# Four buffers instead of two for gathered rows and index columns in the message passing layers of a graph network kernel

## The chip, the cores and the metric

The kernel runs on one core of a Trainium2 chip. The metric is the device time of one execution in microseconds. Before the change it is 11325.51 us, the median of 3 runs (11321.66 to 11331.46).

## What is computed

5000 nodes with 64 features, 165000 edges sorted by their target `dst`, each with 64 features `ea`. Four layers of message passing are followed by a weighted sum over edges. A layer of the reference, cut to what matters:

```python
def _genconv(x, src, dst, ea, W1, b1, lg, lb, W2, b2, t):
    m = relu(x[src] + ea) + EPS          # gather of 165000 rows of 64 floats
    logits = m * t
    mx = segment_max(logits, dst)
    e = exp(logits - mx[dst])
    denom = segment_sum(e, dst)
    agg = segment_sum(m * (e / denom[dst]), dst)
    h = (agg + x) @ W1 + b1
    return relu(_ln(h, lg, lb)) @ W2 + b2
...
ea = edge_attr @ eencW + eencb           # once, for all layers
for i in 1..3: x = x + _genconv(relu(_ln(x)), ...)
```

At the end a second part gathers once more, multiplies with edge weights and sums by target.

## The kernel before, in words

**Windows.** The edges are cut into two halves that are worked side by side (64 features of each half fill the 128 partitions). A window is 1536 edges of each half, 12 tiles of 128. A layer has 52 full windows (`FULLW`) and 4 small ones of half the width (`LAST`), 56 in all (`LW`). Within a window there are three groups (`NG`) of four tiles (`GT`). The number of a window counted over all layers is `g`, within a layer `w`, and `b` is its parity.

**What a window does.** GpSimd gathers the rows of `h_tab` by source with 24 indirect DMAs (12 tiles, 2 halves) into `xg[b]` (line 730), which tell of their landing in `xg_in[b][group]`. TensorE adds, group by group, `ea` times its weights (line 781) and the transposed gathered rows (line 785) in PSUM (`zl`) and counts `z_ps`; ScalarE makes `u` of each group (line 891) and then the logits in `zl` (line 895, `l_ok`). VectorE copies index columns (line 988), and runs the scans: running maximum forward (line 995), backward (line 996), the difference to the logits (line 1001, `diff_ok`), then, after ScalarE's exponentials (line 911), the scans for the denominator `den` (line 1007) and the numerator `num` (line 1011). TensorE transposes both back in six pieces through two PSUM banks (line 800), ScalarE copies each piece to `st_all` (line 903), and SyncE stores the window to `sums`. TensorE issues the forward part of window g+1 before the back part of window g (`layer`, line 804), and ScalarE keeps the same order.

**What GpSimd waits for.** The index columns of all windows lie in `idx_full`, but an indirect DMA takes its columns at a fixed address, so VectorE copies those of window w+2 into `idx[b]` at the start of its work on window w, and counts `idx_ok`. GpSimd waits for that count at the start of a window, and for `z_ps` of the window two before, group by group, which frees the rows' buffer. In the first layer the gathers of window 0 are issued in the block before, and those of window 1 at the start of the layer; in a later layer both wait for the new node table (`tab_out`). The small windows take their columns from `idx_last` and wait for `z_ps` alone.

**Node stage.** After the windows, GpSimd gathers the last sums of each node (`dn`, line 752, 40 indirect DMAs, `dn_in`), and the engines work the two small matrix products, 10 pieces of 4 tiles.

**Lists.** Before layer 0, VectorE also makes five lists for the last part (source, source by tiles, weights, and the two parts of an index), in tiles of their own (`src_i`, `src_n`, `wgt_n`, `lo_t`, `hi_t`); SyncE stores them (`out_lists`). VectorE waits for these stores before the node stage.

Of the kernel before, what the change touches and what calls it, by code (L numbers as in the profile page):

```python
# [25 lines left out]
I32 = mybir.dt.int32  # L26
# [55 lines left out]
def gnn(nc, x, src, dst, edge_attr, edge_weight, encW, encb, eencW, eencb, W1, b1, lnG, lnB, W2, b2,  # L82
# [16 lines left out]
    with ExitStack() as whole:  # L99
        def sb(name, shape, dt=F32, ctx=whole):  # L100
            return ctx.enter_context(nc.sbuf_tensor(name, shape, dt))[tuple([slice(None)] * len(shape))]

        def sem(name):
            return whole.enter_context(nc.semaphore(name))
# [38 lines left out]
        with ExitStack() as c:  # L143
# [60 lines left out]
            with nc.Block() as block:  # L204
                @block.sync
                def _(sp):
# [31 lines left out]
                    for a in acc:  # L238
                        sp.dma_start(a.rearrange("(p t) d -> p (t d)", p=P), zero[:, :]).then_inc(out_tabs, 16)
                    load_lists(2, 2, FULLW)  # L240
                    load_lists(FULLW, 0, 2)
                    sp.wait_ge(out_h, 16 * NC_CHUNK)
# [231 lines left out]
        with ExitStack() as c:  # L474
            xg.append(sb("xg1", [P, K, 2, D], F32, c))
            ea = [sb(f"ea{i}", [P, 2, K, D], F32, c) for i in range(2)]
            at = [sb(f"at{i}", [P, NG, GC], F32, c) for i in range(2)]
            turned = [e.rearrange("p h k d -> p (h k d)").rearrange("p (g c) -> p g c", c=GC) for e in ea]
            idx = [sb(f"idx{i}", [P, 2, K], I32, c) for i in range(2)]
            idx_ok = sem("idx_ok")  # L480
# [76 lines left out]
            XG_LAYER = 32 * GT * FULL_PAIRS + 32 * GT // 2 * (LAST // 2)  # L557

            def xg_count(l, i, gt):
                before = 32 * GT * i if gt == GT else 32 * GT * FULL_PAIRS + 32 * gt * (i - FULL_PAIRS)  # L560
                return l * XG_LAYER + before + 32 * gt

# [7 lines left out]
            with nc.Block() as block:  # L570
# [148 lines left out]
                def _(g_):  # L719

                    def window(g, w, l, b, gt=GT, small=None):
                        if small is None:
                            g_.wait_ge(idx_ok, l * FULLW + w + 1)
                            g_.sem_inc(gather_go, 1)
                        for k in range(NG * gt):
                            if k % gt == 0:
                                g_.wait_ge(z_ps, NG * g + k // gt + 1 - NG * 2 + Z0)
                                g_.sem_inc(gather_go, 1)
                            for h in range(2):
                                g_.indirect_dma_start(xg[b][:, k, h, :], None, h_tab[:, :], bass.IndirectOffsetOnAxis(  # L730
                                    ap=idx[b][:, h, k:k + 1] if small is None else idx_last[:, small, h, k:k + 1],
                                    axis=0)).then_inc(xg_in[b][k // gt], 16)

                    def layer(l):
                        if isinstance(l, int):
                            window(1, 1, l, 1)
                        else:
                            g_.wait_ge(tab_out, 16 * MC * l + 16)
                            g_.sem_inc(gather_go, 1)
                            for b in range(2):  # L740
                                window(l * LW + b, b, l, b)
                        with g_.Fori(1, FULL_PAIRS) as i:
                            for b in range(2):
                                window(l * LW + 2 * i + b, 2 * i + b, l, b)
                        g_.wait_ge(idx_last_in, 16 * LAST_LISTS)
                        for s in range(LAST):
                            window(l * LW + FULLW + s, None, l, s % 2, GT // 2, s)
                        for b in range(2):
# [11 lines left out]
                def _(pe):  # L760
# [3 lines left out]

                    def forward(g, i, l, b, gt=GT):
                        pe.wait_ge(ea_in[b], ea_count(l, i))
# [11 lines left out]
                        for gr in range(NG):  # L778
                            if first:
                                pe.wait_ge(at_sb, NG * g + gr + 1 + A0)  # L780
                            pe.matmul(ps[gr][:, 0:gt * P], attrW[:, :], (at if first else turned)[b][:, gr, 0:gt * P],  # L781
                                      start=True, stop=True)
                            pe.wait_ge(xg_in[b][gr], xg_count(l, i, gt))
                            for j in range(gt):
                                ins = pe.matmul(ps[gr][:, j * P:(j + 1) * P],  # L785
                                                xg[b][:, gr * gt + j, :, :].rearrange("p h d -> p (h d)"), ident[:, :],
                                                start=False, stop=True, skip_group_check=True)
# [16 lines left out]
                    def layer(l):  # L804
                        g0 = l * LW
                        forward(g0, 0, l, 0)
                        with pe.Fori(0, FULL_PAIRS - 1) as i:
                            forward(g0 + 2 * i + 1, i, l, 1)
                            back(g0 + 2 * i, 0)
                            forward(g0 + 2 * i + 2, i + 1, l, 0)  # L810
                            back(g0 + 2 * i + 1, 1)
                        forward(g0 + FULLW - 1, FULL_PAIRS - 1, l, 1)
                        back(g0 + FULLW - 2, 0)
                        for s in range(LAST):
                            forward(g0 + FULLW + s, FULL_PAIRS + s // 2, l, s % 2, GT // 2)
                            back(g0 + FULLW + s - 1, (s - 1) % 2, GT // 2 if s else GT)
# [158 lines left out]
                def _(v):  # L975

                    lists = idx_full.rearrange("p w h k -> p (w h k)")
                    v.wait_ge(idx_full_in, 32)
                    for b in range(2):
                        v.tensor_copy(idx[b].rearrange("p h k -> p (h k)"), lists[:, b * 2 * K:(b + 1) * 2 * K]).then_inc(idx_ok, 1)  # L980
# [8 lines left out]

                    def window(g, w, i, l, b, width=W):  # L990
# [77 lines left out]
                    with v.Fori(0, L) as l:  # L1068
# [14 lines left out]
                        v.tensor_scalar(tcur[:, 1:2], tcur[:, 0:1], EPS, None, ALU.mult).then_inc(tcur_ok, 1)  # L1083
                        with v.Fori(0, FULL_PAIRS) as i:
                            for b in range(2):
                                window(l * LW + 2 * i + b, 2 * i + b, i, l, b)
                        for s in range(LAST):
                            window(l * LW + FULLW + s, FULLW + s, FULL_PAIRS + s // 2, l, s % 2, W // 2)

# [21 lines left out]
                        base = MC * l  # L1111
                        v.wait_ge(out_lists, 16 * 5)
                        for k in range(MC + 3):
                            if k < MC:

                                cs = slice(k * MT, (k + 1) * MT)
                                v.wait_ge(dn_in[k], 16 * MT * (l + 1))
                                if k > 1:
# [493 lines left out]
```

## Time and profile before

| | |
|---|---|
| median of 3 runs | 11325.51 us |
| the profiled execution | 11249.37 us |
| its span | 11247.6 us |
| mean granted clock of TensorE | 0.682 |
| busy: PE 5127.0, DVE 5980.2, ACT 3007.5, POOL 6815.3 us | 46, 53, 27, 61% of the span |
| software queue (gathers), packets' share of 16 engines | 14.1% |
| hardware queue q1 | 22.4% |

Busy time is that of instructions; waits of an engine are the idle time before an instruction, with what ended it ("<-"). "remote" there means that the profile names no instruction as the one that ended the wait; "issue" that it shows no wait. PE is TensorE's matmuls, POOL is GpSimd. The layers lie between 200 and 9050 us, the last part between 9190 us and the end.

### The profile page before, as it was taken

What the parts mean: (1) busy time and instruction counts of PE and PEld (TensorE: products, weight loads), DVE (VectorE), ACT (ScalarE), POOL (GpSimd) and SP (SyncE); (2) the same over time, 40 slices, a digit from 0 to 9 for tenths busy, and PEclk for the clock granted to TensorE, in tenths of its full rate; (3) what the DMA queues carried; (4) which work ended last, traced back from release to release, by engine and by line L of the source; (5) the groups of instructions that cost most, each with busy time, mean ns of one, the idle gap of its engine ahead of it and who ended that gap; (6) DMA issues with size and microseconds to landing.
All of it is one profiled execution on the core that took longest, in us unless ns stands there. A gap on an engine that the chain in (4) does not pass through costs nothing. (4 is left out here: it accounts for less than half of the span.)

```text
span 11247.6 us, 87085 instructions
## 1 busy us (share of the span) xinstructions
PE 5127.0 (46%) x22750; PEld 3577.1 (32%) x22750; DVE 5980.2 (53%) x8070; ACT 3007.5 (27%) x4424; POOL 6815.3 (61%) x6468
## 2 busy tenths in 40 slices
PE   2444444443333332433333334333333358888887
PEld 2333323332222222322222223222222245555554
DVE  4443434443445444535444444444454458888887
ACT  1323223233233232323232323233332331111110
POOL 5554555545656666456666564656566538888887
PEclk8666566666666666666666666665666669999998
DMA  5332333332333333323333332233333335555554
GB/s 137 108 101 97 110 99 99 110 117 57 100 94 104 95 102 87 103 69 104 95 102 97 94 105 76 85 96 103 94 104 95 99 89 97 96 92 97 96 94 83
DMA packets 780499, 1091.38 MB, mean 97 GB/s; under 512 B 501054, under 2 KB 543664, under 8 KB 778660
## 3 DMA queue, kind: packets, MB, share of 16 engines
q1 hardware_dynamic: 453902, 862.82, 22.4%
q0 software_dynamic: 322624, 224.55, 14.1%
q10 hardware_dynamic: 3916, 3.40, 0.1%
q8 instruction: 20, 0.33, 0.0%
q14 instruction: 37, 0.30, 0.0%
HBM read 610.39 MB, written 479.85 MB: 97 GB/s over the span
## 5 line engine op out<-in xcount | busy, mean ns | idle before, releaser
L730 POOL DMA_INDIRECT xg<-h_tab,idx x4968 | 4765.1, 959 | 3546.9 <-DVE idx L988 1870.3
L988 DVE COPY idx<-idx_full 128x24 int32 x208 | 37.6, 181 | 4040.2 <-ACT zl L895 4022.3
L800 PE MATMUL turn<-ident,den 128*128 128x128 f32 x2592 | 492.2, 334 | 3307.1 <-ACT st_all L903 3170.1
L1293 POOL DMA_INDIRECT acc<-vm,tgt x1026 | 1597.6, 1557 | 374.1 <-issue 299.6
L891 ACT ACTIVATE u<-zl,attrB 128x512 f32<-128x512 f32 (+1 forms) x672 | 746.5, 1122 | 3347.6 <-remote 2720.9
L800 PEld LDWEIGHTS turn<-ident,den 128*128 128x128 f32 x2592 | 393.0, 221 | 3357.2 <-ACT st_all L903 3214.9
L785 PEld LDWEIGHTS zl<-ident,xg 128*128 128x128 f32 x5184 | 971.7, 254 | 1122.5 <-issue 993.5
L785 PE MATMUL zl<-ident,xg 128*128 128x128 f32 x5184 | 980.8, 336 | 609.7 <-issue 506.0
L781 PE MATMUL zl<-ea,attrW 128*128 128x512 f32 (+1 forms) x1008 | 752.6, 840 | 793.9 <-DVE rx L1001 751.2
L903 ACT ACTIVATE st_all<-turn 128x512 f32<-128x512 f32 (+1 forms) x1344 | 746.8, 577 | 494.7 <-PE turn L800 324.6
L1542 DVE TENSOR_TENSOR spreadz<-turn,hi_hot 128x2560 f32<-128x2560 f32 x270 | 762.7, 2825 | 65.0 <-ACT gh L1427 26.0
L1366 PE MATMUL zl<-spreadz,lo_hot 128*128 128x512 f32 x1620 | 768.4, 611 | 50.1 <-DVE spreadz L1542 50.1
L995 DVE TENSOR_TENSOR_SCAN rx<-rp,carry,zl 128x1536 f32<-128x1536 bf16 (+1 forms) x224 | 739.8, 3303 | 34.0 <-ACT zl L895 31.7
L1007 DVE TENSOR_TENSOR_SCAN den<-keep,start,rx 128x1536 f32<-128x1536 bf16 (+1 forms) x224 | 739.0, 3299 | 30.3 <-DVE start L1005 0.2
L1011 DVE TENSOR_TENSOR_SCAN num<-keep,start,rx 128x1536 f32<-128x1536 bf16 (+1 forms) x224 | 739.0, 3299 | 7.8
L996 DVE TENSOR_TENSOR_SCAN segmax<-rp,rx 128x1536 f32<-128x1536 bf16 (+1 forms) x224 | 725.6, 3239 | 7.6
L800 PE MATMUL turn<-ident,num 128*128 128x128 f32 x2592 | 599.1, 405 | 100.7 <-issue 70.7
L800 PEld LDWEIGHTS turn<-ident,num 128*128 128x128 f32 x2592 | 485.3, 223 | 178.3 <-ACT st_all L903 80.4
L1366 PE MATMUL rx<-spreadz,lo_hot 128*128 128x512 f32 x1080 | 507.5, 592 | 0.0
L781 PEld LDWEIGHTS zl<-ea,attrW 128*128 128x128 f32 x1008 | 220.0, 271 | 850.5 <-issue 446.8
L781 PE MATMUL zl<-at,attrW 128*128 128x512 f32 (+1 forms) x336 | 290.4, 949 | 381.1 <-ACT at L885 311.1
L885 ACT ACTIVATE at<-turn 128x512 f32<-128x512 f32 (+1 forms) x168 | 93.1, 575 | 1302.0 <-remote 1169.4
(259 smaller groups left out, 7340.9 us busy)
## 6 DMA issues: line engine op xcount, KB each, us to landing
sums<-st_all SPq DMA_DIRECT2D x208, 1536.0 KB
ea<-feat SPq DMA_DIRECT2D x158, 768.0 KB
srcB<-src_flat SPq DMA_DIRECT2D x108, 768.0 KB
rp<-run_pen SPq DMA_DIRECT2D x210, 384.2 KB
xg<-h_tab,idx POOLq DMA_INDIRECT x4968
run_head<-zeros SPq DMA_DIRECT2D x216, 192.0 KB
hd<-run_head SPq DMA_DIRECT2D x108, 384.0 KB
ea<-in_edge_attr_dram SPq DMA_DIRECT2D x104, 384.0 KB
```

Of the source, the lines that this page charges most:

```text
L730: g_.indirect_dma_start(xg[b][:, k, h, :], None, h_tab[:, :], bass.IndirectOffsetOnAxis(ap=idx[b][:, h, k:k + 1] if small is None else idx ...
L781: pe.matmul(ps[gr][:, 0:gt * P], attrW[:, :], (at if first else turned)[b][:, gr, 0:gt * P], start=True, stop=True)
L785: ins = pe.matmul(ps[gr][:, j * P:(j + 1) * P], xg[b][:, gr * gt + j, :, :].rearrange("p h d -> p (h d)"), ident[:, :], start=False, stop= ...
L800: ins = pe.transpose(ps[6 + (b + r) % 2][:, j * P:(j + 1) * P], sum_v[:, gr * gt + j, :], ident[:, :])
L891: a.activation(u[b][:, 0:width].rearrange("c (p k) -> c k p", k=NG * gt)[:, gr * gt:(gr + 1) * gt, :], ps[gr][:, 0:gt * P].rearrange("c (k ...
L903: a.activation(st[b].rearrange("p h k c -> p k h c")[:, gr * gt:(gr + 1) * gt, :, s_ * D:(s_ + 1) * D], ps[6 + (b + r) % 2][:, 0:gt * P].r ...
L995: link(v.tensor_tensor_scan(rx[:, 0:width], rp[b][:, 0:width], zl[:, 0:width], carry[:, 0:1], ALU.min, ALU.max))
L1007: v.tensor_tensor_scan(den[b][:, 0:width], keep[b][:, 0:width], rx[:, 0:width], start2[:, 0:1], ALU.mult, ALU.add).then_inc(den_ok, 1)
L1011: v.tensor_tensor_scan(num[b][:, 0:width], keep[b][:, 0:width], rx[:, 0:width], start2[:, 1:2], ALU.mult, ALU.add).then_inc(sums_ok, 1)
L1293: g_.indirect_dma_start(acc[i][:, :], bass.IndirectOffsetOnAxis(ap=tgt[b][:, t_:t_ + 1], axis=0), vm[b][:, t_, :], None, compute_op=ALU.ad ...
L1366: ins = pe.matmul(bank[:, :], lo_hot[b][:, n, :], z[:, part * 512:(part + 1) * 512], start=False, stop=True, skip_group_check=True)
L1542: v.tensor_tensor(spreadz[(XT * b + n) % 2][:, :, :], rows_bank[2][:, at_:at_ + D].unsqueeze(1).broadcast_to([P, NT, D]), hi_hot[b][:, n, ...
```

## The change

The tiles for gathered rows and for index columns become four each (`DEPTH`). VectorE copies the columns of window w+4 at the start of window w, GpSimd waits for `z_ps` of the window four before, gathers windows 1 to 3 at the start of layer 0 and windows 0 to 3 at that of a later layer, and the loops of TensorE, VectorE and GpSimd cover four windows a turn in place of two. `ea`, `rp`, `u`, `den`, `num` and the store's buffers stay double. The room for it comes from the five lists' tiles, which now lie in `segmax`, `den` and `num`; so the wait for the lists' stores moves from the node stage to the point before the first `den` scan of every window. The ten semaphores of the node rows are taken from the twelve of the gathered rows, with their counts added.

```diff
+        DEPTH = 4
-        idx_full = sb("idx_full", [P, FULLW + 2, 2, K], I32)
+        idx_full = sb("idx_full", [P, FULLW + DEPTH, 2, K], I32)
-        xg_in = [[sem(f"xg_in{i}_{gr}") for gr in range(NG)] for i in range(2)]
+        xg_in = [[sem(f"xg_in{i}_{gr}") for gr in range(NG)] for i in range(DEPTH)]
...
-                    load_lists(0, 0, 2)
+                    load_lists(0, 0, DEPTH)
...
-            xg.append(sb("xg1", [P, K, 2, D], F32, c))
+            xg += [sb(f"xg{i}", [P, K, 2, D], F32, c) for i in range(1, DEPTH)]
-            idx = [sb(f"idx{i}", [P, 2, K], I32, c) for i in range(2)]
+            idx = [sb(f"idx{i}", [P, 2, K], I32, c) for i in range(DEPTH)]
...
-            src_i = sb("src_i", [ROWS, W], I32, c)
-            src_n = sb("src_n", [ROWS, W], F32, c)
-            wgt_n = sb("wgt_n", [ROWS, W], F32, c)
+            src_i = segmax[0:ROWS, :].bitcast(I32)
+            src_n = den[0][0:ROWS, :]
+            wgt_n = den[1][0:ROWS, :]
...
-            lo_t = sb("lo_t", [ROWS, W], F32, c)
-            hi_t = sb("hi_t", [ROWS, W], F32, c)
+            lo_t = num[0][0:ROWS, :]
+            hi_t = num[1][0:ROWS, :]
...
-            dn_in = [sem(f"dn_in{i}") for i in range(MC)]
...
-            Z0, U0, L0, M0, S0, BP0, BS0, A0, D0 = 2 * NG, NG, 2, 2, 2, 2 * BU, BU + 1, 2, 1
+            Z0, U0, L0, M0, S0, BP0, BS0, A0, D0 = DEPTH * NG, NG, 2, 2, 2, 2 * BU, BU + 1, 2, 1
...
+            dn_in = [xg_in[n // NG][n % NG] for n in range(MC)]
...
                         for k in range(NG * gt):
                             if k % gt == 0:
-                                g_.wait_ge(z_ps, NG * g + k // gt + 1 - NG * 2 + Z0)
+                                g_.wait_ge(z_ps, NG * g + k // gt + 1 - NG * DEPTH + Z0)
...
-                        if isinstance(l, int):
-                            window(1, 1, l, 1)
-                        else:
+                        if not isinstance(l, int):
                             g_.wait_ge(tab_out, 16 * MC * l + 16)
                             g_.sem_inc(gather_go, 1)
-                            for b in range(2):
-                                window(l * LW + b, b, l, b)
-                        with g_.Fori(1, FULL_PAIRS) as i:
-                            for b in range(2):
-                                window(l * LW + 2 * i + b, 2 * i + b, l, b)
+                        for b in range(1 if isinstance(l, int) else 0, DEPTH):
+                            window(l * LW + b, b, l, b)
+                        with g_.Fori(1, FULLW // DEPTH) as i:
+                            for b in range(DEPTH):
+                                window(l * LW + DEPTH * i + b, DEPTH * i + b, l, b)
...
                         if width == W:
-                            next_lists(w + 2, b)
+                            next_lists(w + DEPTH, place)
...
                         v.wait_ge(back_ps, BU * (g - 1) + BP0)
+                        v.wait_ge(out_lists, 16 * 5)
                         v.tensor_tensor_scan(den[b][:, 0:width], keep[b][:, 0:width], rx[:, 0:width], start2[:, 0:1],
                                              ALU.mult, ALU.add).then_inc(den_ok, 1)
```

## Rows read from the trace of the kernel before

**Rows 1.** The page's costliest groups: count, busy us, mean ns, idle before, releaser.
```profile
L730 POOL DMA_INDIRECT xg<-h_tab,idx x4968 | 4765.1, 959 | 3546.9 <-DVE idx L988 1870.3
L988 DVE COPY idx<-idx_full 128x24 int32 x208 | 37.6, 181 | 4040.2 <-ACT zl L895 4022.3
```

**Rows 2.** Stretches, layers 0 and 1: us; busy (count) PE, PEld, DVE, ACT, POOL; PEclk, DMA, GB/s.
```profile
201.50:2502.00 2300.50, 1025.23 (x5407) 758.39 (x5408) 983.01 (x726) 687.38 (x886) 1194.46 (x1248) 0.63 0.33 104
2662.00:4682.90 2020.90, 670.52 (x2894) 501.20 (x2895) 983.07 (x724) 612.92 (x721) 1210.05 (x1265) 0.62 0.33 98
```

**Rows 3.** Timeline of one window in layer 1: start us, duration, what.
```profile
3029.86 0.18 DVE L988 COPY idx<-idx_full 128x24 int32 x1 [17.91 <-ACT zl L895]
3031.03 0.96 POOL L730 DMA_INDIRECT xg<-h_tab,idx  x1 [7.91 <-DVE idx L988]
...
3042.67 1.16 ACT L891 ACTIVATE u<-zl,attrB 128x512 f32<-128x512 f32 x1 [0.97 <-PE zl L785]
...
3045.69 1.05 PE L785 MATMUL zl<-ident,xg 128*128 128x128 f32 x8
...
3060.05 0.95 POOL L730 DMA_INDIRECT xg<-h_tab,idx  x1 [0.30 <-issue]
3064.75 1.14 ACT L891 ACTIVATE u<-zl,attrB 128x512 f32<-128x512 f32 x1 [11.46 <-remote]
...
3067.73 0.18 DVE L988 COPY idx<-idx_full 128x24 int32 x1 [17.91 <-ACT zl L895]
```

**Rows 4.** Timeline of ScalarE, back part of a window near layer 1's end.
```profile
4480.85 0.60 ACT L903 ACTIVATE st_all<-turn 128x512 f32<-128x512 f32 x1 [9.90 <-remote]
...
4500.45 0.60 ACT L903 ACTIVATE st_all<-turn 128x512 f32<-128x512 f32 x1 [7.80 <-remote]
...
4516.84 0.60 ACT L903 ACTIVATE st_all<-turn 128x512 f32<-128x512 f32 x1 [0.36 <-PE turn L800]
```

**Rows 5.** Timelines of GpSimd, VectorE and ScalarE at the start of layer 2.
```profile
4802.07 1.27 POOL L730 DMA_INDIRECT xg<-h_tab,idx  x1 [62.79 <-issue]
...
4840.94 3.45 DVE L995 TENSOR_TENSOR_SCAN rx<-rp,carry,zl 128x1536 f32<-128x1536 bf16 x1
...
4892.00 0.96 POOL L730 DMA_INDIRECT xg<-h_tab,idx  x1 [0.31 <-issue]
...
4893.18 1.15 ACT L891 ACTIVATE u<-zl,attrB 128x512 f32<-128x512 f32 x1 [25.44 <-remote]
...
4906.08 3.42 DVE L995 TENSOR_TENSOR_SCAN rx<-rp,carry,zl 128x1536 f32<-128x1536 bf16 x1
```

**Rows 6.** Stretches, one full window (w50 of layer 1).
```profile
4591.30:4611.40 20.10, 10.80 (x50) 7.99 (x49) 18.06 (x15) 10.89 (x12) 10.84 (x12) 0.75 0.46 149
```

**Rows 7.** Stretches, layer 1: w46 to w49; w47; w49; w46 to the end.
```profile
4433.10:4591.30 158.20, 53.30 (x225) 38.70 (x226) 72.26 (x53) 46.25 (x55) 97.72 (x103) 0.61 0.30 94
4463.60:4515.20 51.60, 14.07 (x64) 10.32 (x65) 18.01 (x14) 12.90 (x17) 24.43 (x26) 0.60 0.23 70
4536.00:4591.30 55.30, 16.66 (x63) 11.89 (x64) 17.98 (x14) 12.33 (x16) 36.64 (x40) 0.56 0.26 72
4433.10:4682.90 249.80, 99.21 (x426) 74.94 (x427) 147.73 (x126) 89.81 (x128) 137.82 (x144) 0.65 0.36 108
```

**Rows 8.** Stretches, layer 0: w47 to the end; 44 windows in its middle.
```profile
2267.10:2502.00 234.90, 117.50 (x661) 91.68 (x662) 130.07 (x115) 88.95 (x139) 114.86 (x120) 0.68 0.39 122
332.00:2267.00 1935.00, 854.81 (x4472) 628.76 (x4472) 794.51 (x570) 559.96 (x700) 1008.43 (x1054) 0.62 0.32 103
```

**Rows 9.** Timeline of VectorE, last small window of layer 1.
```profile
4671.66 1.82 DVE L995 TENSOR_TENSOR_SCAN rx<-rp,carry,zl 128x768 f32<-128x768 bf16 x1
4682.93 0.22 DVE L1092 CUSTOM_DVE_ANT_0 wjunk<-wmax,win_hot 128x56 f32<-128x56 f32 x1 [0.20 <-DVE carry L1015]
```

**Rows 10.** Timeline at the start of layer 0.
```profile
202.54 0.95 POOL L730 DMA_INDIRECT xg<-h_tab,idx  x1 [26.28 <-DVE idx L988]
...
212.46 3.41 DVE L1007 TENSOR_TENSOR_SCAN den<-keep,start,rx 128x1536 f32<-128x1536 bf16 x1 [0.15 <-DVE start L1005]
```

More of the change, by code:

```diff
@@ L239, in _ @@
                         sp.dma_start(a.rearrange("(p t) d -> p (t d)", p=P), zero[:, :]).then_inc(out_tabs, 16)
-                    load_lists(2, 2, FULLW)
-                    load_lists(FULLW, 0, 2)
+                    load_lists(DEPTH, DEPTH, FULLW)
+                    load_lists(FULLW, 0, DEPTH)
                     sp.wait_ge(out_h, 16 * NC_CHUNK)
@@ L551, in gnn, with xg_count, dn_count @@
             LAST_LISTS = sum(E - h * HALF - FULLW * W - s * W // 2 > 0 for s in range(LAST) for h in range(2))
-            Z0, U0, L0, M0, S0, BP0, BS0, A0, D0 = 2 * NG, NG, 2, 2, 2, 2 * BU, BU + 1, 2, 1
+            Z0, U0, L0, M0, S0, BP0, BS0, A0, D0 = DEPTH * NG, NG, 2, 2, 2, 2 * BU, BU + 1, 2, 1
             PAIRS = LW // 2
             FULL_PAIRS = FULLW // 2
[L557 to L561, printed above, removed]
+            XG_LAYER = 32 * GT * FULLW // DEPTH + 32 * GT // 2 * LAST // DEPTH
+            dn_in = [xg_in[n // NG][n % NG] for n in range(MC)]
+            def xg_count(l, turn_, gt, n):
+                before = 32 * GT * turn_ if gt == GT else 32 * GT * FULLW // DEPTH
+                return l * (XG_LAYER + (16 * MT if n < MC else 0)) + before + 32 * gt
+            def dn_count(l):
+                return (l + 1) * (XG_LAYER + 16 * MT)
             def ea_count(l, i):
@@ L734, in layer @@
                     def layer(l):
-                        if isinstance(l, int):
-                            window(1, 1, l, 1)
-                        else:
+                        if not isinstance(l, int):
                             g_.wait_ge(tab_out, 16 * MC * l + 16)
                             g_.sem_inc(gather_go, 1)
-                            for b in range(2):
-                                window(l * LW + b, b, l, b)
-                        with g_.Fori(1, FULL_PAIRS) as i:
-                            for b in range(2):
-                                window(l * LW + 2 * i + b, 2 * i + b, l, b)
+                        for b in range(1 if isinstance(l, int) else 0, DEPTH):
[3 more added lines that the diff above has]
+                                window(l * LW + DEPTH * i + b, DEPTH * i + b, l, b)
                         g_.wait_ge(idx_last_in, 16 * LAST_LISTS)
                         for s in range(LAST):
-                            window(l * LW + FULLW + s, None, l, s % 2, GT // 2, s)
+                            window(l * LW + FULLW + s, None, l, s, GT // 2, s)
                         for b in range(2):
@@ L763, in _, with forward @@
                     pe.sem_inc(back_ps, BP0)
-                    def forward(g, i, l, b, gt=GT):
+                    def forward(g, i, l, b, turn_, place, gt=GT):
                         pe.wait_ge(ea_in[b], ea_count(l, i))
@@ L782, in forward @@
                                       start=True, stop=True)
-                            pe.wait_ge(xg_in[b][gr], xg_count(l, i, gt))
+                            pe.wait_ge(xg_in[place][gr], xg_count(l, turn_, gt, NG * place + gr))
                             for j in range(gt):
                                 ins = pe.matmul(ps[gr][:, j * P:(j + 1) * P],
-                                                xg[b][:, gr * gt + j, :, :].rearrange("p h d -> p (h d)"), ident[:, :],
+                                                xg[place][:, gr * gt + j, :, :].rearrange("p h d -> p (h d)"), ident[:, :],
                                                 start=False, stop=True, skip_group_check=True)
@@ L805, in layer @@
                         g0 = l * LW
[L806 to L813, printed above, removed]
+                        forward(g0, 0, l, 0, 0, 0)
+                        with pe.Fori(0, FULLW // DEPTH - 1) as i:
+                            for n in range(1, DEPTH + 1):
+                                forward(g0 + DEPTH * i + n, DEPTH // 2 * i + n // 2, l, n % 2, i + n // DEPTH, n % DEPTH)
+                                back(g0 + DEPTH * i + n - 1, (n - 1) % 2)
+                        for n in range(FULLW - DEPTH + 1, FULLW):
+                            forward(g0 + n, n // 2, l, n % 2, n // DEPTH, n % DEPTH)
+                            back(g0 + n - 1, (n - 1) % 2)
                         for s in range(LAST):
-                            forward(g0 + FULLW + s, FULL_PAIRS + s // 2, l, s % 2, GT // 2)
+                            forward(g0 + FULLW + s, FULL_PAIRS + s // 2, l, s % 2, None, s, GT // 2)
                             back(g0 + FULLW + s - 1, (s - 1) % 2, GT // 2 if s else GT)
@@ L978, in _ @@
                     v.wait_ge(idx_full_in, 32)
-                    for b in range(2):
+                    for b in range(DEPTH):
                         v.tensor_copy(idx[b].rearrange("p h k -> p (h k)"), lists[:, b * 2 * K:(b + 1) * 2 * K]).then_inc(idx_ok, 1)
@@ L988, in next_lists, with window @@
                         v.tensor_copy(idx[b].rearrange("p h k -> p (h k)"), lists[:, bass.ds(w * 2 * K, 2 * K)]).then_inc(idx_ok, 1)
-                    def window(g, w, i, l, b, width=W):
+                    def window(g, w, i, l, b, place, width=W):
                         link = Chain(v, dve_step, g * STEPS)
@@ L1083, in _ @@
                         v.tensor_scalar(tcur[:, 1:2], tcur[:, 0:1], EPS, None, ALU.mult).then_inc(tcur_ok, 1)
-                        with v.Fori(0, FULL_PAIRS) as i:
-                            for b in range(2):
-                                window(l * LW + 2 * i + b, 2 * i + b, i, l, b)
+                        with v.Fori(0, FULLW // DEPTH) as i:
+                            for n in range(DEPTH):
+                                window(l * LW + DEPTH * i + n, DEPTH * i + n, DEPTH // 2 * i + n // 2, l, n % 2, n)
                         for s in range(LAST):
-                            window(l * LW + FULLW + s, FULLW + s, FULL_PAIRS + s // 2, l, s % 2, W // 2)
+                            window(l * LW + FULLW + s, FULLW + s, FULL_PAIRS + s // 2, l, s % 2, None, W // 2)
                         v.wait_ge(dve_step, (l + 1) * LW * STEPS)
@@ L1111, in _ @@
                         base = MC * l
-                        v.wait_ge(out_lists, 16 * 5)
                         for k in range(MC + 3):
@@ L1116, in _ @@
                                 cs = slice(k * MT, (k + 1) * MT)
-                                v.wait_ge(dn_in[k], 16 * MT * (l + 1))
+                                v.wait_ge(dn_in[k], dn_count(l))
                                 if k > 1:
```

## The prediction

> **What bounds the kernel now.** I read the page's groups first, then the stretches, then the timeline of one window, and then the places where the timeline departs from its pattern. The group of the gathers [rows 1] shows GpSimd busy for 4765 us and idle for 3547 us before gathers, 1870 us of it "released by" the DVE copy of index columns (L988). Layer 0 takes 2300.5 us from its first scan to its last window, layer 1 takes 2020.9 [rows 2], and layers 2 and 3 are like layer 1; together some 8360 of 11248 us, so this is where the change acts.
>
> One window in the middle of layer 1 lasts 37.9 us [rows 3]. At 3029.86 DVE copies the index columns; 1.2 us later GpSimd begins 24 gathers, one every 1.264 us, and issues the last at 3060.05 (30.3 us in all); then it is idle for 7.9 us until the next copy. The copy at the start of window w hands over the columns of w+2, so the gathers of this stretch are for the window after next. The next window's rows already lie in the other buffer. PE shows this: it issues that window's group 2 at 3045.69, in the middle of the stream. But ScalarE reads group 0 at 3042.67 and group 2 only at 3064.75, 19 us after PE issued it, with "remote" as releaser, while ScalarE, DVE and PE have nothing else to do. The logits and the next copy at 3067.73 follow. The last u starts 3.7 us after the end of the last gather's issue (3060.05 + 0.96). So the chain of a window is: copy, 1.2 us, gather stream 30.3 us, 3.7 us, u and logits 3.0 us, copy.
>
> Why does a window wait for gathers that it doesn't read? The same happens where gathered rows play no part. In the transposes of sums (L800), PE's results reach ScalarE in 0.3 to 0.4 us when no gathered rows are landing, and 8 to 10 us apart while GpSimd streams: ScalarE's idle time before st_all is 9.90 and 7.80 us in one stretch (a piece between them is the same), 0.36 us in a quiet one [rows 4]. My reading: while gathered rows land, what PE has finished is reported late, and what is pending comes out mostly when the stream pauses. The page "TensorE: Matmul & The Clock Gate" of the Trainium skill, section "The cost: per-tile semaphore tail", has PE's increments cost about 26 ns each; rows 4 disagree by two orders of magnitude in the stream and agree only outside it. By that page nothing would hold the windows but GpSimd, which is rival D below.
>
> The start of a layer shows a stream with no pause [rows 5]. GpSimd starts at 4802.07 and streams three windows (w0, w1, w2) to 4892.96. Window 0's scan starts at 4840.94, but the second piece of window 1's u comes at 4893.18, after 25.44 us of waiting and just as the stream ends, and the scan at 4906.08: 65.1 us for one window. A window whose passes meet few gathers takes 20.1 us [rows 6]. So streaming further ahead isn't free: it is paid in late windows while it lasts.
>
> **The change, part by part.** (1) Four buffers and four index columns. The copy in window w hands over w+4, and GpSimd waits for z_ps of w rather than of the window two back from its own target; both are again "window w has passed". In the steady state the ring is full, GpSimd waits for the copy of window w, and that copy starts one window of gathers (w+4 in place of w+2). The chain of rows 3 is the same term by term: 1.2 + 30.3 + 3.7 + 3.0, 38 us. It is worth nothing there. I bound it: at most the 7.9 us of idle per window (rival D), and at worst the stop-and-go pattern (rival E).
>
> (2) The start of layers 1 to 3. GpSimd now issues w0 to w3 at once, and w4 as soon as window 0 has passed: the stream ends (k+4) x 30.33 us after its start, if window k is the one whose end it must await. Window k then can be held until about 8 us after it (6.7 us in rows 3, 13.1 us in rows 5). Before, scans start 38.9 and 104.0 us [rows 5] after the first gather, then every 37.9 us. For k = 1: 160 against 104, 56 us late; k = 2: 190 against 142, 48; k = 3: 221 against 180, 41; k = 6: 311 against 294, 18. Which k depends on how fast windows pass in a stream; rows 5 have one in 65 us, and the stretches with a stream in most of them 51.6 and 55.3 us [rows 7]. At 65 us window 2 would pass at 169 and window 3 at 234, past the 221 of k = 3; I take 45 us, between k = 2 and 3.
>
> (3) The end of each layer. GpSimd is two windows further ahead, so it finishes earlier and two more windows run at 20.1 in place of 37.9. From the scan of w47: gathers of w51 to 31.5 us, two groups of the first small window to 41.6, 6.7 us to the next scan, 48; then four windows at 20 and four small ones at 11.3 (layer 1's last, [rows 9]): 173 us. The small windows' gathers (15 us each) start when a z group is done and fall beside DVE's scans, as at 4591 to 4611, where one took 20.1 us with 12 gathers in it. Before, from the scan of w46, 249.8 us [rows 7]; now 37.9 + 173 = 211, so 39 us are won. Bounds: 0 and 50.
>
> (4) Layer 0. GpSimd gathers w1 until 176.3 us and is then idle for 26.3 us until the first copy [rows 10]. Now w2 and w3 follow at once and stream to 237; window 0's z groups fall into that stream. Window 0 can be held to 245 (44 us late), window 1 to 275 against 241 (34 us). I take 35. At the end, from w47's scan 234.9 us before [rows 8]; now some 54 + 4 x 21 + 4 x 13 = 190 (an estimate: the terms of (3), each with a little of the 6 us that a window of layer 0 takes longer), 45 us less. Together -10.
>
> (5) The wait for the list stores, now before the first den scan, which began at 212.46 [rows 10]: it is met long before in later windows, and DVE waits for the logits in each. Were it late in window 0 alone, it would cost what the stores need, 0 to 10 us once; I take 0. Scratch in the rooms of sums and maxima moves no instruction. Two more columns loaded early and two more copies of 0.18 us: nothing. Shared semaphores for node rows: same transfers, same order. Longer loop bodies: ScalarE's and SyncE's keep two windows; no row prices the others, I take 0, with 0 to 10 us per layer.
>
> The sum: 3 x (45 - 39) - 10 = +8 us on the profiled execution's 11249.4 us. That execution is 76 us faster than the runs' median of 11325.5, which says that the irregular stretches vary between executions; I carry the difference over: 11334 us, said as 11335.
>
> **The rivals.** What a measurement can tell from no change is 0.2%, 23 us.
> B, slower: the start decides. If PE's results hardly come out in a stream, window 1 is held until GpSimd has filled the ring (k = 1 in layers 1 to 3, k = 0 in layer 0): 3 x (56 - 39) + (44 - 45) = +50, 11376 us; with the win at the end halved it is +131, 11456. It decides from 47 us of start cost per layer on. For it: the 25.44 us before a piece of u in the unbroken stream of rows 5. Against: pieces 8 to 11 us apart in rows 4.
> C, somewhat faster: windows pass in about 45 us in the stream, so that the ring fills slowly (k = 6): 3 x (18 - 39) + (0 - 45) = -108, 11217 us. For it: 51.6 and 55.3 us were mostly stream, not wholly bad. Against: 65.1.
> D, much faster: GpSimd's issue becomes the bound, 30.3 us a window, no idle time before copies: 46 windows x 3 x 7.6, and 46 x 13.7 in layer 0 (whose middle windows take 1935.0 / 44 = 44.0 us [rows 8]), 1680 us less, 9645 us. It needs PE's lateness to be something that goes when the gathers are further ahead, say a wait for the rows themselves. For it: the 1870 us in rows 1, read plainly. Against: rows 4, where no gathered row is read, and PE's own group 2 issued at 3045.69.
> E, slower by a pattern: four windows near the end of layer 1, two of them 51.6 and 55.3 us, make 158.2 for 4 x 37.9 = 151.6 [rows 7]; were it the rule with more room to run ahead, 208 / 4 x 6.6 = +343, 11669 us.
> That the change doesn't do what it says (the ring never used beyond two) would be exactly the old time and belongs to the forecast.
>
> **How the numbers follow.** Forecast 0.33, B 0.30, C 0.18, D 0.10, E 0.09. The likeliest case's own range is 11290 to 11380. Within 23 us of before lies 0.27 (most of the forecast and the edges of B and C); slower 0.38 (B, E and a piece of the forecast's upper side, less B's lower edge); faster 0.35 (C, D and the forecast's lower side). The range, 11215 to 11460, takes in B with the halved gain and C, and leaves out D and E, about 2 in 10.
>
> **What the profile after would show.** Right: middle windows again 37.9 us (44 in layer 0), idle time before gathers about as before and still put down to the copy of index columns, group 2's u still some 3.7 us after the stream's end; at the layers' starts one stream of six or so windows with windows 1 to 3 taking 50 to 75 us each; at the ends four or five windows of 20 us in a row. The forecast falls if middle windows shrink towards 30.3 us, if u's idle time "remote" (L891) vanishes, or if the starts cost less than 20 us or more than 60. The window-0 wait is wrong if DVE stands before den at 212 us.

## The result: 0.63% slower, and two kinds of chip

The changed kernel takes 11402.78 us (median of 4 runs, 11399.75 to 11406.66) against 11328.49 us (4 runs): ratio 1.0063, 95% interval 1.005 to 1.0076, 74 us slower. Its profiled execution takes 11400.83 us (span 11399.1), 2 us from its median; that of the old kernel was 76 us below its own.

The experiments brought a second result. On three chips the old kernel took 9127.8 to 9137.4 us, on two others 11321.3 and 11323.7, each in at least 7 runs that lay within 0.3%. I call the latter kind A; the runs above are of it by their times. The others are kind B. There the changed kernel is 0.17% faster. Each of the five chips showed one kind in all its executions, but four of them in one sitting only, so a lasting state of a chip is not told from the chip itself. What follows first is kind A.

**The profile after.** The page's groups, as in [rows 1], with the group of u; columns: count, busy us, mean ns, idle before, releaser:

```profile
L734 POOL DMA_INDIRECT xg<-h_tab,idx x4968 | 4760.8, 958 | 3537.2 <-DVE idx L990 1873.6
L990 DVE COPY idx<-idx_full 128x24 int32 x208 | 37.7, 181 | 4103.3 <-ACT zl L897 3928.1
L893 ACT ACTIVATE u<-zl,attrB 128x512 f32<-128x512 f32 (+1 forms) x672 | 750.8, 1122 | 3379.9 <-remote 2557.9
```

GpSimd's idle time is in total what it was (3546.9 us before), and has the same releaser. Twice the buffers took 10 us from it. One window in layer 2 answers to [rows 3]:

```profile
5224.92 0.18 DVE L990 COPY idx<-idx_full 128x24 int32 x1 [18.32 <-ACT zl L897]
5226.09 0.95 POOL L734 DMA_INDIRECT xg<-h_tab,idx  x1 [8.09 <-DVE idx L990]
...
5237.73 1.15 ACT L893 ACTIVATE u<-zl,attrB 128x512 f32<-128x512 f32 x1 [0.96 <-PE zl L787]
...
5241.15 1.05 PE L787 MATMUL zl<-ident,xg 128*128 128x128 f32 x8
...
5250.23 1.14 ACT L893 ACTIVATE u<-zl,attrB 128x512 f32<-128x512 f32 x1 [11.35 <-remote]
...
5255.06 0.95 POOL L734 DMA_INDIRECT xg<-h_tab,idx  x1 [0.30 <-issue]
5260.07 1.15 ACT L893 ACTIVATE u<-zl,attrB 128x512 f32<-128x512 f32 x1 [8.70 <-remote]
5263.05 0.18 DVE L990 COPY idx<-idx_full 128x24 int32 x1 [18.11 <-ACT zl L897]
```

Copy, 1.2 us, 24 gathers, 4.1 us, last u, logits, copy: 38.1 us. The second piece of u comes 12.5 us after the first, the third 9.8 us after that. The start of layer 1 answers to [rows 5]; timelines of all engines:

```profile
2633.78 0.95 POOL L734 DMA_INDIRECT xg<-h_tab,idx  x1 [64.25 <-issue]
...
2658.95 1.15 ACT L893 ACTIVATE u<-zl,attrB 128x512 f32<-128x512 f32 x1 [8.93 <-PE zl L787]
...
2671.64 1.14 ACT L893 ACTIVATE u<-zl,attrB 128x512 f32<-128x512 f32 x1 [11.54 <-issue]
...
2700.42 1.14 ACT L893 ACTIVATE u<-zl,attrB 128x512 f32<-128x512 f32 x1 [13.95 <-PE zl L787]
...
2727.02 1.14 ACT L893 ACTIVATE u<-zl,attrB 128x512 f32<-128x512 f32 x1 [25.46 <-issue]
...
2755.72 1.14 ACT L893 ACTIVATE u<-zl,attrB 128x512 f32<-128x512 f32 x1 [27.55 <-remote]
...
2778.12 0.60 ACT L905 ACTIVATE st_all<-turn 128x512 f32<-128x512 f32 x1 [11.30 <-remote]
2778.77 1.13 PE L802 MATMUL turn<-ident,num 128*128 128x128 f32 x4 [10.76 <-issue]
...
2788.62 0.60 ACT L905 ACTIVATE st_all<-turn 128x512 f32<-128x512 f32 x1 [9.90 <-remote]
...
2801.43 1.91 PE L783 MATMUL zl<-ea,attrW 128*128 128x512 f32 x2
...
2815.52 0.95 POOL L734 DMA_INDIRECT xg<-h_tab,idx  x1 [0.30 <-issue]
...
2837.12 2.96 ACT L893 ACTIVATE u<-zl,attrB 128x512 f32<-128x512 f32 x3 [12.13 <-remote]
...
2841.92 0.18 DVE L990 COPY idx<-idx_full 128x24 int32 x1 [8.89 <-ACT zl L897]
2842.01 3.42 DVE L997 TENSOR_TENSOR_SCAN rx<-rp,carry,zl 128x1536 f32<-128x1536 bf16 x1
2842.32 1.14 PE L802 MATMUL turn<-ident,den 128*128 128x128 f32 x4 [4.56 <-ACT st_all L905]
2843.09 0.95 POOL L734 DMA_INDIRECT xg<-h_tab,idx  x1 [26.61 <-DVE idx L990]
```

GpSimd streams six windows without waiting for a copy, 2633.8 to 2816.5, and then waits 26.61 us for the copy. The last two pieces of window 0's u are 12.7 us apart, those of window 1's 27 and 29; those of st_all, which has fewer matmuls in a piece, 10.5 to 12. The stretches, columns as in [rows 2]: layer 1 from its first gather to window 2's scan, on to w47's scan (45 windows), and to its end; layer 0 to window 2's scan, and from w47's scan to its end:

```profile
2633.80:2842.00 208.20, 36.77 (x120) 24.24 (x120) 39.44 (x33) 27.09 (x27) 139.10 (x144) 0.54 0.18 42
2842.00:4562.20 1720.20, 563.68 (x2430) 421.58 (x2430) 814.51 (x586) 513.35 (x586) 1030.90 (x1080) 0.61 0.32 98
4562.20:4741.80 179.60, 87.47 (x372) 67.61 (x373) 129.59 (x114) 79.24 (x115) 68.72 (x72) 0.68 0.39 121
100.50:331.80 231.30, 47.78 (x268) 34.31 (x268) 91.15 (x130) 31.84 (x36) 149.77 (x144) 0.57 0.42 113
2326.20:2512.30 186.10, 108.76 (x660) 86.94 (x661) 129.52 (x113) 90.16 (x139) 68.70 (x72) 0.71 0.44 146
```

### The profile page after: what moved, and what is told of

It reads as the page before. It is cut to its first block and busy times, and to the rows that moved or that the text cites. A ratio compares the mean times of both kernels' runs of the same rounds, so it can differ in the third digit from the quotient of the medians.

```text
span 11399.1 us, 86751 instructions
## 1 busy us (share of the span) xinstructions
PE 5130.5 (45%) x22750; PEld 3585.2 (31%) x22750; DVE 5970.2 (52%) x8072; ACT 3009.9 (26%) x4424; POOL 6809.2 (60%) x6468
## 5 line engine op out<-in xcount | busy, mean ns | idle before, releaser
L990 DVE COPY idx<-idx_full 128x24 int32 x208 | 37.7, 181 | 4103.3 <-ACT zl L897 3928.1
L1010 DVE TENSOR_TENSOR_SCAN den<-keep,start,rx 128x1536 f32<-128x1536 bf16 (+1 forms) x224 | 739.0, 3299 | 44.3 <-issue 35.3
L1368 PEld LDWEIGHTS zl<-spreadz,lo_hot 128*128 128x128 f32 x1620 | 299.3, 199 | 366.7 <-issue 272.9
```

Of the source, the lines that this page charges most:

```text
L1368: ins = pe.matmul(bank[:, :], lo_hot[b][:, n, :], z[:, part * 512:(part + 1) * 512], start=False, stop=True, skip_group_check=True)
```

## The experiments

**One part at a time: how far GpSimd runs ahead.** Buffers and loop bodies stay as changed. Two windows ahead is this edit, in the first copies of index columns, the later ones, and the count that GpSimd waits for; three and one have a 3 and a 1 in it.

```
-                    for b in range(DEPTH):
+                    for b in range(2):
-                            next_lists(w + DEPTH, place)
+                            next_lists(w + 2, (place + 2) % DEPTH)
-                                g_.wait_ge(z_ps, NG * g + k // gt + 1 - NG * DEPTH + Z0)
+                                g_.wait_ge(z_ps, NG * g + k // gt + 1 - NG * 2 + Z0)
```

> The changed kernel with its four buffers, loop bodies and waits, but GpSimd runs only two windows ahead again: the copy in window w hands over w+2, and both the first copies and GpSimd's wait for z_ps count two windows. Theory T (what PE has finished is reported late while gathered rows land, so running further ahead costs at each start and pays at each end): the old time, 11330 us (11310 to 11345); windows after a layer's first scan 64 and 38 us, layer ends two windows at 20 us again. Rival F (the new form costs: longer loop bodies, one more wait in each window, shared semaphores): stays at 11380 to 11410.

Measured: 9137.92 us beside an old kernel of 9129.07, ratio 1.001 (1.0001 to 1.0019). It landed on kind B, so neither number of the expectation could be met, and nothing followed for the 74 us. The same holds for the next three.

> As the run with two windows ahead, but three. T: between them, 11350 to 11380 us: starts of layers 1 to 3 some 30 to 35 us longer than with two, ends about 18 us per layer shorter, middle windows 38 us. Rival F: 11380 to 11410, the same for two, three and four.

Measured: 9114.49, ratio 0.9984 (0.9975 to 0.9993).

Waiting once for the stores of the lists, ahead of the loop over layers, in place of in window() before the den scan:

```
-                        v.wait_ge(out_lists, 16 * 5)
+                    v.wait_ge(out_lists, 16 * 5)
```

> The changed kernel, with the wait for the list stores once ahead of the layers in place of once in each window. Forecast's step 5 (that wait costs nothing): 11403 us within 10, middle windows 38.2 us as now. Rival: the wait carries the 0.25 us by which middle windows grew (38.2 against 37.95): then some 11 us per layer go, 11355 to 11365 us.

Measured: 9126.82, ratio 0.9996 (0.9987 to 1.0005), beside 0.9983 with the wait in the window (below). VectorE's timeline of this run:

```profile
178.51 0.06 DVE L1073 MEMSET carry<- 128x1 f32 x1 [8.33 <-DMA hi_tile<-num]
...
194.63 0.18 DVE L990 COPY idx<-idx_full 128x24 int32 x1 [12.10 <-ACT zl L897]
```

DVE stands 8.33 us at the wait, and the first scan comes at 194.7 us where the changed kernel has it at 185.7. In the window the wait is met when VectorE comes to it: in the changed kernel DVE is idle for 0.22 us before the first den on kind B and on kind A alike (0.15 us before the change [rows 10]), and before all 224 den scans together for 44.3 us where the old kernel's page has 30.3. That is 14 us more in four layers, so the rival's 11 us in each can't be idle time of that wait, even on kind A, where this edit was not run.

Rows two windows ahead, index columns four (only the third pair of lines of the edit above):

> The changed kernel with its index columns four windows ahead, but GpSimd's wait for z_ps counts two windows: rows of w+2 are gathered as soon as w's z group is reported, not after w's logits. If the late copy were what held GpSimd (the 1874 us of its idle time put down to it), windows go to 30 to 33 us and the kernel below 10500 us. T: GpSimd's stream then comes in three pieces of 10 us, each held by a z group that the piece before it makes late: 13 + 14 + 14 us, 38 to 42 us a window, 11300 to 12100 us.

Measured: 9134.5, ratio 1.0004 (0.9995 to 1.0013). On kind B neither what holds the rows nor what holds the lists matters to middle windows, 30.2 us here too. But the changed kernel's 0.17% is gone with the rows' lead: it goes with rows four windows ahead, not with index columns.

**The changed and the old kernel on kind B.**

> The changed kernel as it is, once more, because in the four runs before the old kernel took 9129 us in place of 11328. Theory T2 (whether PE's results are late in a gather stream depends on the chip, not on the kernel): where the old kernel takes some 9130 us, its windows take 30.3 us, which is GpSimd's issue, and the change makes no difference: ratio 0.998 to 1.001; where the old kernel takes some 11330 us, the ratio is 1.006 again. Rival: the change costs 70 us wherever it runs (the form of the code), ratio 1.008.

Measured: 9122.02 against 9137.35, ratio 0.9983 (0.9974 to 0.9992): as the theory had it for this kind, against the rival's 1.008.

> The old kernel itself, for its profile on a chip where it takes some 9130 us. T2 (GpSimd's issue is the bound there): all full windows of layers 1 to 3 at 30.3 us, GpSimd with next to no idle time within them, 3 windows of some 23 us at the start of layer 0 where the changed kernel has 6; the 15 us between the two kernels lie in layer 0. Should the time be 11330 us, the profile is the first one's again, with windows of 38 us.

Measured: 9129.27, ratio 1.0 (0.9989 to 1.0012). The middle of layer 1 in this run, and its groups:

```profile
1956.50:3316.30 1359.80, 710.06 (x2430) 496.02 (x2430) 814.13 (x587) 512.77 (x586) 1030.70 (x1081) 0.63 0.42 124
```

```profile
L730 POOL DMA_INDIRECT xg<-h_tab,idx x4968 | 4752.6, 957 | 1628.1 <-issue 1584.4
L785 PE MATMUL zl<-ident,xg 128*128 128x128 f32 x5184 | 1200.4, 405 | 1552.7 <-DMA xg<-h_tab,idx 1541.7
...
L891 ACT ACTIVATE u<-zl,attrB 128x512 f32<-128x512 f32 (+1 forms) x672 | 758.3, 1128 | 2620.9 <-PE zl L785 2620.6
```

45 windows in 1359.8 us are 30.2 us each: GpSimd's issue. The idle time before the gathers that was put down to the copy of index columns is gone, PE waits for the rows to land, and "remote" has vanished before u. What the change can win here is the start of layer 0. GpSimd's timelines, old kernel and changed kernel; the listed rows are those with an idle time of over 1 us before them:

```profile
120.90 0.95 POOL L730 DMA_INDIRECT xg<-h_tab,idx  x1 [6.83 <-DVE idx L980]
187.86 0.95 POOL L730 DMA_INDIRECT xg<-h_tab,idx  x1 [27.20 <-DVE idx L988]
```

```profile
121.37 0.96 POOL L734 DMA_INDIRECT xg<-h_tab,idx  x1 [6.84 <-DVE idx L982]
```

The 27.20 us are gone, and window 6 is scanned at 324.7 us in place of 346.5. Layers 1 to 3 give back 3.7, 4.8 and 5.3 us (1652.8, 1653.9 and 1654.7 from first gather to last window, against 1649.1, 1649.1 and 1649.4).

**Taking away half of the gathers.**

```
-                            for h in range(2):
+                            for h in range(2 if small is not None else 1):
                                 g_.indirect_dma_start(xg[b][:, k, h, :], ...
```

Not shown: the counts that PE and VectorE wait for follow it, and the buffers are zeroed once before layer 0. The kernel leaves out the second half's rows.

> The changed kernel with 12 gathers in a full window in place of 24 (the second half's rows aren't gathered; small windows and all other work stay). GpSimd's stream is then 15.2 us a window. If the chip is one on which the old kernel takes some 9130 us and GpSimd's issue is the bound: windows fall to 20.1 us (23 in layer 0), the time of a window without that bound, some 7280 us. If it is one on which it takes some 11330: T gives 15.2 + 7.7 = 23 us a window (29 in layer 0), some 8400 us; a rival in which the lateness doesn't depend on gathers leaves windows at 38.

Measured, on kind B: 7235.07, ratio 0.7923 (0.7909 to 0.7936). Windows of 20.1 to 21 us (20.45 on average) and 22 to 23.7 in layer 0, as said.

**One window ahead.**

> The changed kernel with GpSimd one window ahead. On a chip of 9130 us: nothing lies between a window's last gather and the window any more, and the chain is copy, 1.2, 30.3, landing 2.4, PE 1.1, u 1.1, logits 1.6 = 37.7 us: +7.4 a window, some 10600 us. On a chip of 11330 us, T: windows take the same chain already, 38 us as with two and four, starts of layers shorter by some 28 us and ends longer by 18: 11300 us within 60; a rival in which work done in the stream counts: 45 to 50 us a window, over 12500 us.

Measured, on kind B: 10710.43, ratio 1.1728 (1.1709 to 1.1748); all middle windows 37.7 us, the sum of the chain as worked out; the total is 110 us over what was said. One buffer of lead hides the gathers behind nothing; with two everything but GpSimd's issue is hidden, and a third and fourth have nothing left to hide.

**Four windows ahead in layer 0, two later.**

```
-                                g_.wait_ge(z_ps, NG * g + k // gt + 1 - NG * DEPTH + Z0)
+                                g_.wait_ge(z_ps, NG * g + k // gt + 1 - NG * (DEPTH if isinstance(l, int) else 2) + Z0)
                             g_.wait_ge(idx_ok, l * FULLW + w + 1)
+                            if not isinstance(l, int):
+                                g_.wait_ge(l_ok, g - 2 + 1 + L0)
```

> The changed kernel, GpSimd four windows ahead in layer 0 and two from layer 1 on (it waits there for the logits of the window two back). On a chip of 9130 us: as the changed kernel, ratio 0.998, since what the change wins there is in layer 0, where GpSimd doesn't stand idle before window 0's copy. On a chip of 11330 us, T: layers 1 to 3 as in the old kernel (2061 to 2070 us), layer 0 as in the changed one (+10): 11340 us, ratio 1.001.

Measured, on kind B: 9111.43, ratio 0.998 (0.997 to 0.999), the number expected: the win is layer 0's. It was not run on kind A.

**The same kernels on kind A.** First two windows ahead:

> The changed kernel with GpSimd two windows ahead once more, sent because the runs so far all had the old kernel at 9129 to 9137 us. Should the old kernel take some 11330 us beside it, T (the depth of running ahead costs at the starts) expects ratio 1.000 to 1.002 and layer starts of 64 and 38 us, rival F (the form costs) 1.005 to 1.008. Beside an old kernel of 9130 us it repeats the first ratio, 1.001, and tells nothing of the 11330 us.

Measured: 11332.89 (11325.67 to 11338.55) against 11323.65, ratio 1.0009 (1.0 to 1.0019). The changed kernel had 1.0063. Rival F's 1.005 to 1.008 is out: of the 0.63%, 0.54% (61 us) go with the depth alone. A small price of the form is left: this same kernel has 1.0009 here and 1.001 (1.0001 to 1.0019) on kind B. The start of layer 1 to window 2's scan and from w47's scan to the end, in this run:

```profile
2644.70:2788.60 143.90, 32.54 (x120) 22.79 (x120) 39.52 (x35) 27.55 (x27) 93.48 (x96) 0.58 0.21 51
4504.10:4722.90 218.80, 90.45 (x372) 69.29 (x373) 129.82 (x113) 78.93 (x115) 114.74 (x120) 0.62 0.37 106
```

Next to the changed kernel's stretches: 208.2 against 143.9, 64.3 us lost at the start; 179.6 against 218.8, 39 us won at the end.

> 12 gathers in a full window in place of 24, once more (second half's rows not gathered), for a chip on which the old kernel takes 11330 us. There, T (PE's results wait for gathered rows to stop landing): a window is its stream of 15.2 us and the 7.7 us behind it, 23 us, some 29 in layer 0, 8400 us in all. Rival (the lateness has nothing to do with the gathers): windows of 38 us, 11300 us. Rival (half the landings are few enough that nothing is late): 20.3 us, 7300 us. On a chip of 9130 us it repeats 7235.

Measured: 8040.19, ratio 0.7102 (0.7088 to 0.7116). The middle of layer 1:

```profile
1888.70:2888.20 999.50, 554.52 (x2430) 416.13 (x2430) 815.18 (x586) 503.78 (x586) 515.30 (x540) 0.70 0.46 151
```

45 windows of 22.2 us, 27.4 in layer 0: the stream of 15.2 us and 7.0 behind it, 0.8 less than said; the total is 360 us less than said. The rival of 38 us is out: with half of the gathers the late windows go. The one of 20.3 us misses by 1.9 us, T by 0.8, and since the same kernel has 20.45 on kind B, the middle windows tell these two apart by little. The layer's start does it better: the scans of windows 0 and 1 are 66.1 us apart here and 20.1 on kind B. So at both lengths tried the stream and some 7 to 8 us behind it make a middle window of layers 1 to 3 on kind A.

> GpSimd one window ahead, once more, for a chip on which the old kernel takes 11330 us. There, T with nothing of use done in a stream: windows of 38 us as with two and four, starts of layers 28 us shorter than with two, ends 18 longer: 11300 us within 60. Rival, that a window's passes use the stream (some 12 of its 20 us beside it): 45 to 50 us a window, over 12500 us. On a chip of 9130 us it repeats 10710.

Measured: 11376.7 (11358.92 to 11377.06), ratio 1.0044 (1.0027 to 1.006), 17 us over the upper end of T's 11300 within 60. Start, middle and end of layer 1:

```profile
2663.00:2777.80 114.80, 39.21 (x120) 25.48 (x120) 39.70 (x34) 27.48 (x27) 70.58 (x72) 0.60 0.23 57
2777.80:4505.90 1728.10, 754.33 (x2430) 501.68 (x2430) 814.32 (x587) 511.17 (x586) 1033.68 (x1080) 0.59 0.32 97
4505.90:4750.70 244.80, 105.84 (x372) 74.66 (x373) 129.87 (x114) 79.33 (x115) 137.84 (x144) 0.60 0.34 98
```

The start is 29.1 us shorter than with two, as expected, the end 26.0 longer (18 expected), and 0.28 us more per middle window makes 12.7. The windows of 38.4 us don't support T by themselves: on kind B the same kernel has 37.7, from the chain of landing rows.

For layers 1 to 3 the depth is then priced on kind A, all in the same form of the kernel (us, from the scans):

```
windows ahead   first gather to w2's scan   w47's scan to the end   layer 0, first gather to end
1               114.8 114.6 114.4           244.8 248.9 250.7       2442.9
2               143.9 145.2 145.1           218.9 218.8 218.2       2422.8
4               208.2 209.3 209.3           179.5 181.3 175.4       2411.8
```

Two is the best of them on kind A; no version that ran beats the old kernel there, and on kind B three, four and the mixed one beat it by 0.16 to 0.2%.

## Why the prediction was right in part

The time, 11402.78, lies in the range given and 68 us above the number; it is outside the likeliest case's own range (11290 to 11380) and in rival B's, 11376 to 11456. B was the case of a start that costs more than 47 us per layer; it did. B's own way there (window 1 held until the ring is full, k = 1) isn't what happened: window 1 passes within the stream, and window 2 is held. So the number lies near B's by another way.

**The steady state, part (1)**: right. 38.1 to 38.2 us, put down to the same copy, the last u 4.1 us after the stream.

**The start of layers 1 to 3, part (2), is the step that failed.** It had 45 us; against the same form with two windows ahead it is 64 (64.3, 64.1 and 64.2), against the old kernel's profile 66 to 67 (141.9 to window 2's scan in each of its layers). The stream's length was right: (2 + 4) x 30.33 = 182 us for k = 2, and it took 182.7. Two terms were wrong. The smaller is which window is held: I took 45 us as the cost, between the 48 of k = 2 and the 41 of k = 3, going by 65.1 us for a window in a stream [rows 5]. The stream's end had cut that window short; in the long stream it takes 84.1 (2674.7 to 2758.8), so it is window 2. That is 3 us. The larger is what comes behind the stream: I had window 2 pass "about 8 us after it", and it passed 25.5 us after it, which is the other 18.

The reading behind it was not sharp enough. I had PE's results "reported late", with no price. In the long stream the gaps scale with the matmuls in a piece, not with the reports: a piece of u is 2 + 8 matmul instructions, a piece of st_all 4 (x2, x8, x4 in the rows above), and they come 26.6 to 28.7 us and 10.5 to 11.9 us apart: 2.6 to 3.0 us a matmul in both. The 25.44 us of waiting in the old kernel [rows 5], with the some 1.2 us of the piece before it, are the same rate. The PE rows give another picture (x8 in 1.05 us), but by what ScalarE is given, PE works off one matmul per some 2.7 us there. It isn't the price wherever rows land: window 0's last pieces at the head of the same stream are 12.7 us apart (18.5 and 17.0 in layers 2 and 3), and the first two of a middle window 12.5 (above): 1.3 to 1.9 us a matmul at most, beside gathers issued at the same pace. Why it rises later in a stream was not tried. With the 2.7 us, taken from this profile and so after the fact, the term comes out: window 1's 30 matmuls are 81 us (84.1 with the rest of the window); window 2 has the 24 transposes of window 0 ahead of its own 30, 146 us, more than the 57.7 left of the stream, so it passes behind it, with nearly all of its 30 still to do. All three pieces can be read some 15 us after the last st_all (2821.6 to 2837.1), half a us a matmul, so what was held is worked off once the stream is over. Whether PE is slow in starting, reading or finishing them isn't told apart.

**The end, part (3)**: right. 39 us; measured 39.4, 37.5 and 42.8. From w47's scan 173; measured 175 to 181.

**Layer 0, part (4)**: the net is right, -10 against -11.0, and both halves are 10 us larger: +44.7 at the start (231.3 against 186.6 to window 2's scan) and -55.8 at the end (186.1 from w47's scan, where the text had 190, against 241.9 with two windows ahead, where it had 234.9).

**Part (5)**: right within its bounds. The wait finds its stores done. The form costs 0.09% on kind A, 9 us, at the edge of its interval.

With these terms the sum is 3 x (64 - 40) - 11 = +61 us, the 0.54% between the two depths; the form's 9 us make it 70 of the 74. Carrying over the 76 us by which the old kernel's profiled execution was fast was right: 11321 to 11328 in all comparisons on kind A. Its middle windows had 37.8 to 37.9 us, while both kernels of the new form have 38.2; whether the old one has 38.2 in an ordinary execution wasn't seen.

**Rival D** (GpSimd's issue as the bound, 30.3 us a window) is false on kind A and describes kind B well, but there it is the state of the old kernel too, and not something that the change brings. I had not thought of the chip as a condition. The rule weighed there (the Trainium skill, "TensorE: Matmul & The Clock Gate", "The cost: per-tile semaphore tail": some 26 ns per increment) is likewise at odds with kind A's rows only: on kind B transposes reach their reader in 0.26 us beside a stream (last rows below). No run measures an increment itself, on either kind.

## What to carry to other kernels

Deeper prefetch is worth something only where the prefetching engine stands idle for want of a buffer in its steady state: if its idle time has the same releaser with the ring full, more depth moves the irregular ends alone, and starts and ends are to be priced apart. When results reach their reader in slow steps, count the instructions in each step before calling it latency, and check the price in a second place: here 2.7 us a matmul fits two kinds of pieces in a long stream, and not those at its head. And a verdict of under one per cent belongs to the chips it was taken on: this one changes its sign between them.

## What was unexpected in the hardware

Two groups of chips run one program 24% apart (11321 to 11328 against 9128 to 9137 us), each steady within 0.3%. The transfers' packets don't take longer: the rows on gathered rows' queue, old kernel, kind A and then kind B,

```profile
q0 software_dynamic: 322624, 224.55, 14.1%
```

```profile
q0 software_dynamic: 322624, 224.55, 17.2%
```

make 0.141 x 11247.6 = 1586 us and 0.172 x 9128.6 = 1570 us of the 16 engines' time. The clock granted to PE in middle windows is the same too (0.62 in [rows 2], 0.63 on kind B). What differs is PE's work beside landing rows. On kind B, at the start of layer 2 (old kernel, ScalarE's timeline), window 1's three pieces of u are 6.9 and 7.7 us apart, where kind A has 27 to 29, and a transposed piece comes 0.26 us after the one before it was read:

```profile
3640.46 1.16 ACT L891 ACTIVATE u<-zl,attrB 128x512 f32<-128x512 f32 x1 [0.90 <-PE zl L785]
3647.38 1.15 ACT L891 ACTIVATE u<-zl,attrB 128x512 f32<-128x512 f32 x1 [5.76 <-PE zl L785]
3655.04 1.17 ACT L891 ACTIVATE u<-zl,attrB 128x512 f32<-128x512 f32 x1 [6.51 <-PE zl L785]
...
3660.46 0.60 ACT L903 ACTIVATE st_all<-turn 128x512 f32<-128x512 f32 x1 [0.26 <-PE turn L800]
```

The traces differ in one more thing: that of the old kernel holds 52,230 changes of semaphores on kind A and 143,621 on kind B; with two windows ahead it is 51,128 and 143,565. On kind A that can't be all of them: the kernel counts 16 for each gather, and 4968 gathers alone make 79,488. So on kind A the trace lacks records, which may be why so many waits there are "remote"; the starts of instructions, on which the readings above rest, are read without them. Two guesses fit this. One is a path of semaphore changes that is clogged on kind A while rows land, each gather bringing its own increments; no run varied the increments and left the rows. The other is that the recording of the profile itself holds the program there: the executions on record have a recorded span and clock beside their times, so none shows the program without it. What makes a chip of one kind or the other stays open too.
